# Tanh-weighted gate and product with up on VectorE, weight alone on GpSimd, transposes and key projection moved

## What is computed

```python
x = x + attn(layernorm(x))        # q, k, v projections, softmax in a band of 64, output projection
h = layernorm(x)                  # then the experts:
g = einsum('nh,ehm->enm', h, w_gate)      # 16 experts, 64 hidden
u = einsum('nh,ehm->enm', h, w_up)
inter = silu(g) * u
y_e = einsum('enm,emh->enh', inter, w_down)
y = einsum('ne,enh->nh', combine, y_e)    # combine: routing weight of each token and expert
shared = (silu(h @ sw_gate) * (h @ sw_up)) @ sw_down
x = x + y + shared
```

## Time and profile before

| | |
|---|---|
| median of 3 runs | 814.77 us (814.01 to 815.94) |
| the profiled execution | 814.36 us, span 812.6 us |
| TensorE busy, weight loads | 740.3 us (91%), 611.7 us (75%) |
| GpSimd | 618.8 us (76%) |
| ScalarE | 607.7 us (75%) |
| VectorE | 525.1 us (65%) |
| mean granted clock | 0.977 |
| chain of waits that ended last | PE 45%, POOL 26%, issue 16%, ACT 8% |

### The profile page before, as it was taken

How to read it: one execution, slowest core, us unless ns; L and a number is a source line. 1 busy time by engine, 2 the same in 40 slices (tenths; PEclk the granted TensorE clock), 3 DMA queues, 4 the chain that set the end, 5 groups by cost and what they waited for, 6 DMA issues and landing times.

```text
span 812.6 us, 19809 instructions
## 1 busy us (share of the span) xinstructions
PE 740.3 (91%) x5984; PEld 611.7 (75%) x5984; DVE 525.1 (65%) x1735; ACT 607.7 (75%) x1816; POOL 618.8 (76%) x842
## 2 busy tenths in 40 slices
PE   2568889999999999999999999999999999998876
PEld 1446668787887878787887878787887878786755
DVE  3456686767767676767667676767767575764332
ACT  4787788788787888878788788878787888863332
POOL 3525467879888888978888888988888887956876
PEclk9698899999999999999999999999999999999999
DMA  5000022040413213040312213040313203041321
GB/s 155 26 1 15 14 74 73 15 136 10 120 40 97 63 53 105 2 133 22 105 52 92 65 42 115 2 129 26 105 52 90 67 31 114 3 122 37 117 92 41
DMA packets 50738, 53.86 MB, mean 66 GB/s; under 512 B 5632, under 2 KB 31744, under 8 KB 50560
## 3 DMA queue, kind: packets, MB, share of 16 engines
q1 hardware_dynamic: 50688, 53.25, 21.5%
HBM read 44.31 MB, written 4.72 MB: 60 GB/s over the span
## 4 chain that ended last, share of the span: by engine, by line
PE 45%; POOL 26%; issue 16%; ACT 8%; DMA 2%; DVE 2%; POOLq 1%; SPq 0%; ACTq 0%; DVEq 0%
POOL gate L470 9%; PE PS L1053 8%; PE PS L979 7%; PE PS L869 7%; PE PS L911 6%; PE PS L870 5%; PE PS L871 5%; ACT probs L602 4%; POOL hh L473 4%; POOL q_lo L452 4%; POOL k_lo L462 2%; PE PS L972 2%; PE PS L1050 2%; POOL X L432 1%; PE PS L1014 1%
## 5 line engine op out<-in xcount | busy, mean ns | idle before, releaser
L602 ACT ACTIVATE probs<-PS,neg_max 128x96 f32<-128x96 f32 (+1 forms) x1024 | 245.8, 353 | 60.1 <-DVE neg_max L798 59.4
L470 POOL TENSOR_TENSOR gate<-gate,spread 128x512 f32<-128x512 f32 x128 | 164.2, 1283 | 64.4 <-DMA spread<-weights_by_expert 47.2
L750 DVE STREAM_TRANSPOSE probsT<-probs 128x384 f32<-128x384 f32 (+1 forms) x256 | 124.0, 522 | 101.8 <-ACT probs L602 101.8
L473 POOL TENSOR_TENSOR hh<-gate,tu 128x512 f32<-128x512 f32 x128 | 164.5, 1285 | 17.2 <-POOL gate L470 11.9
L786 DVE SCALAR_TENSOR_TENSOR tu<-th,PS 128x512 f32<-128x512 f32 x128 | 87.9, 687 | 89.3 <-PE PS L871 56.4
L1053 PE MATMUL PS<-wd,hh 128*128 128x128 f32 x1024 | 136.1, 276 | 9.6 <-POOL hh L473 9.6
L1053 PEld LDWEIGHTS PS<-wd,hh 128*128 128x128 f32 x1024 | 126.6, 192 | 15.1 <-POOL hh L473 9.4
L798 DVE TENSOR_REDUCE neg_max<-PS 128x4 f32<-128x384 f32 (+1 forms) x256 | 125.4, 513 | 8.2 <-PE PS L979 5.4
L869 PE MATMUL PS<-x_hi,w_hi 128*128 128x512 f32 x288 | 125.0, 434 | 1.0 <-DVE hs L834 1.0
L560 ACT ACTIVATE th<-PS 128x512 f32<-128x512 f32 x128 | 79.7, 623 | 59.6 <-PE PS L871 59.2
L871 PE MATMUL PS<-x_lo,w_hi 128*128 128x512 f32 x288 | 114.5, 397 | 0.0
(11 more groups left out here) (108 smaller groups left out, 1362.1 us busy)
## 6 DMA issues: line engine op xcount, KB each, us to landing
spread<-weights_by_expert SPq DMA_DIRECT2D x256, 128.0 KB, 3.0
X<-x SPq DMA_DIRECT2D x32, 256.0 KB, 3.4
OUT<-H SPq DMA_DIRECT2D x16, 256.0 KB, 3.0
out<-OUT SPq DMA_DIRECT2D x16, 256.0 KB, 3.1
probsT<-w_gu SPq DMA_DIRECT2D x1, 1152.0 KB, 8.0
wd<-w_down SPq DMA_DIRECT2D x1, 512.0 KB, 9.0
weights_by_expert<-cT SPq DMA_DIRECT2D x16, 32.0 KB, 1.6
probsT<-w_att SPq DMA_DIRECT2D x1, 264.0 KB, 3.5
```

Source lines behind the costliest of these rows:

```text
L470: tt(gate2[:, :], gate[:, k % 2, :], spread[:, k % SP_BUFS, :], ALU.mult).then_inc(s_g2, 1)
L473: tt(hh[:, k % 2, :], gate2[:, :], tu[:, k % 2, :], ALU.mult).then_inc(s_h, 1)
L602: ins = nc.scalar.activation(probs[:, u % 2, tt, a, j0:KW], PS[:, tt, a * KW + j0:a * KW + KW], ACT.Exp, bias=neg_max[:, tt, a:a + 1])
L750: ins = v_.transpose(probsT[:, b, :, t0 + tt, c0:3, :].rearrange("p g c q -> p g (c q)"), probs[:, u % 2, tt, :, c0 * Q:KW])
```

## The change

The pair's activation is split in another way. ScalarE doesn't copy the gate any more. VectorE computes fa = (th + 1) * gate, reading the gate from PSUM, and then tu = fa * up, reading up from PSUM. GpSimd multiplies once: hh = tu * spread. The tiles `gate` and `gate2` and their semaphores go, and with them TensorE's wait on `s_gate`; `s_fa` now counts every pair, and ScalarE waits on it before it writes `th` again.

In step 3 TensorE computes the shared experts' gate and up ahead of the weights' transposes instead of behind them; ScalarE's tanh of the shared experts and its copy to `cT` change places in the same way.

The key projection is done once for both sequences, in step 6, into a whole bank (512 columns); `kr_hi` and `kr_lo` become twice as wide, and the uses of the shared banks go from 15 to 14 in a slot.

```diff
-KP = (6, 8)
+KP = 6
@@ gpsimd, the pair
-                        pool.wait_ge(s_gate, g.n * NP + k + 1)
                         pool.wait_ge(s_spread[k % SP_BUFS], spread_turn(g, k))
-                        tt(gate2[:, :], gate[:, k % 2, :], spread[:, k % SP_BUFS, :], ALU.mult).then_inc(s_g2, 1)
-                        pool.wait_ge(s_g2, g.n * NP + k + 1)
                         pool.wait_ge(s_tu, g.n * NF + k + 2)
-                        tt(hh[:, k % 2, :], gate2[:, :], tu[:, k % 2, :], ALU.mult).then_inc(s_h, 1)
+                        tt(hh[:, k % 2, :], tu[:, k % 2, :], spread[:, k % SP_BUFS, :], ALU.mult).then_inc(s_h, 1)
@@ scalar, the pair
                         act.wait_ge(s_g, g.n * NF + k + 2)
+                        act.wait_ge(s_fa, g.n * NF + k + 1)
                         nc.scalar.activation(th[:, :], PS[:, 4, :], ACT.Tanh, scale=0.5).then_inc(s_th, 1)
-                        copy(gate[:, k % 2, :], PS[:, 4, :]).then_inc(s_gate, 1)
@@ vector, the pair
-                        dve.wait_ge(s_th, g.n * NF + k + 2)
-                        dve.wait_ge(s_u, g.n * NF + k + 2)
-                        v_.scalar_tensor_tensor(tu[:, k % 2, :], th[:, :], 1.0, PS[:, 5, :], ALU.add,
-                                                ALU.mult).then_inc(s_tu, 1)
+                        f = g.n * NF + k + 2
+                        dve.wait_ge(s_th, f)
+                        v_.scalar_tensor_tensor(fa[:, :], th[:, :], 1.0, PS[:, 4, :], ALU.add,
+                                                ALU.mult).then_inc(s_fa, 1)
+                        dve.wait_ge(s_fa, f)
+                        dve.wait_ge(s_u, f)
+                        v_.tensor_tensor(tu[:, k % 2, :], fa[:, :], PS[:, 5, :], ALU.mult).then_inc(s_tu, 1)
@@ tensor, gate_up
-                if not (g.fixed and g.n * NP + f <= 1):
-                    pe.wait_ge(s_gate, g.n * NP + max(f - 1, 0))
@@ tensor, keys: one call in place of keys(0) and keys(1)
-                            exact3(bank[:, 0:T], *w2(WK), xT_hi[:, r], xT_lo[:, r]).then_inc(s_filled[side], 1)
+                        exact3(bank, *w2(WK), xT_hi[:, :], xT_lo[:, :]).then_inc(s_filled[side], 1)
@@ tensor, step 3
+                    g, _ = at(sl, s, SH)
+                    if g:
+                        gate_up(g, NP, 0)
+
                     g, _ = at(sl, s, CT)
...
-                    g, _ = at(sl, s, SH)
-                    if g:
-                        gate_up(g, NP, 0)
-
-                    keys(1)
```

More of the change, by code:

```diff
@@ L187, in preln_block_kernel @@
         q_lo = sb("q_lo", [P, NSB, 4, Q], F32R)
-        kr_hi = sb("kr_hi", [P, T], F32R)
-        kr_lo = sb("kr_lo", [P, T], F32R)
+        kr_hi = sb("kr_hi", [P, TOK], F32R)
+        kr_lo = sb("kr_lo", [P, TOK], F32R)
         k_hi = sb("k_hi", [P, HG, TOK], F32R)
@@ L223, in preln_block_kernel @@
         fa = sb("fa", [P, TOK])
-        gate = sb("gate", [P, 2, TOK])
         tu = sb("tu", [P, 2, TOK])
@@ L542, in slot @@
                         copy(w_hi[:, WG:W_COLS], stage[:, WG:W_COLS]).then_inc(s_cst, 1)
-                    def keys(b):
-                        g, _ = at(sl, s, KP[b])
-                        if g:
-                            side, bank = filled(act, sl, s, KEY_PLACE[b])
-                            if not (g.fixed and g.n == 0 and b == 0):
-                                act.wait_ge(s_k_hi, g.n * GB + b)
-                            copy(kr_hi[:, :], bank[:, 0:T]).then_inc(s_high[side], 1)
-                    keys(0)
+                    g, _ = at(sl, s, KP)
+                    if g:
+                        side, bank = filled(act, sl, s, EARLY)
+                        if not (g.fixed and g.n == 0):
+                            act.wait_ge(s_k_hi, g.n * GB)
+                        copy(kr_hi[:, :], bank).then_inc(s_high[side], 1)
                     g, _ = at(sl, s, LG)
@@ L566, in slot @@
                         copy(oT[:, :], bank[:, 0:T]).then_inc(s_taken[side], 1)
+                    g, _ = at(sl, s, SH)
+                    if g:
+                        act.wait_ge(s_g, g.n * NF + 1)
+                        if not (g.fixed and g.n == 0):
+                            act.wait_ge(s_fa, g.n * NF)
+                        nc.scalar.activation(th[:, :], PS[:, 4, :], ACT.Tanh, scale=0.5).then_inc(s_th, 1)
                     g, _ = at(sl, s, CT)
@@ L572, in slot @@
                         copy(cT[:, :], bank[0:E, :], scale=0.5 * ROUTE_SCALE).then_inc(s_taken[side], 1)
-                    g, _ = at(sl, s, SH)
-                    if g:
-                        act.wait_ge(s_g, g.n * NF + 1)
-                        if not (g.fixed and g.n == 0):
-                            act.wait_ge(s_fa, g.n)
-                        nc.scalar.activation(th[:, :], PS[:, 4, :], ACT.Tanh, scale=0.5).then_inc(s_th, 1)
-                    keys(1)
                     g, _ = at(sl, s, QP)
@@ L627, in slot @@
                         if g:
[L628 removed]
+                            if b == 0:
+                                taken(act, sl, KP, EARLY)
                             if not (g.fixed and g.n == 0):
@@ L632, in slot @@
                             for a in range(HG):
-                                ins = copy(k_hi[:, a, T * b:T * b + T], kr_hi[:, :].bitcast(F32),
+                                ins = copy(k_hi[:, a, T * b:T * b + T], kr_hi[:, T * b:T * b + T].bitcast(F32),
                                            scale=headrow[:, a:a + 1])
@@ L761, in slot @@
                                      ).then_inc(s_taken[side], 1)
-                    def keys(b):
-                        g, _ = at(sl, s, KP[b])
-                        if g:
-                            side, bank = high_out(sl, s, KEY_PLACE[b])
-                            if not (g.fixed and g.n == 0 and b == 0):
-                                dve.wait_ge(s_k_lo, HG * (g.n * GB + b))
-                            split_low(kr_lo[:, :], bank[:, 0:T], kr_hi[:, :]).then_inc(s_taken[side], 1)
                     g, _ = at(sl, s, YE)
@@ L775, in slot @@
                                          ALU.add).then_inc(s_y, 1)
-                    keys(0)
+                    g, _ = at(sl, s, KP)
+                    if g:
+                        side, bank = high_out(sl, s, EARLY)
+                        if not (g.fixed and g.n == 0):
+                            dve.wait_ge(s_k_lo, HG * g.n * GB)
+                        split_low(kr_lo[:, :], bank, kr_hi[:, :]).then_inc(s_taken[side], 1)
                     g, _ = at(sl, s, LN1)
@@ L923, in free @@
                         return use.bank, PS[:, RING[use.bank], :]
-                    def keys(b):
-                        g, _ = at(sl, s, KP[b])
-                        if g:
-                            side, bank = free(KEY_PLACE[b])
-                            r = slice(T * b, T * b + T)
-                            exact3(bank[:, 0:T], *w2(WK), xT_hi[:, r], xT_lo[:, r]).then_inc(s_filled[side], 1)
-                    keys(0)
+                    g, _ = at(sl, s, KP)
+                    if g:
+                        side, bank = free(EARLY)
+                        exact3(bank, *w2(WK), xT_hi[:, :], xT_lo[:, :]).then_inc(s_filled[side], 1)
                     g, _ = at(sl, s, VP)
```

22 lines of the change are left out of this document (7 added, 15 removed).

## The result

| | before | changed |
|---|---|---|
| median | 814.44 us (4 runs, 814.01 to 815.94) | 883.07 us (4 runs, 880.42 to 891.53) |
| ratio to before, 95% interval | | 1.086 (1.078 to 1.093) |
| profiled execution | 814.36 us, span 812.6 us | 880.42 us, span 878.6 us |
| one full slot | 46.0 us | 49.1 to 50.4 us, two of 54.03 and 58.07 |
| mean granted clock | 0.977 | 0.948 |

The change costs 8.6%. I had forecast 854 us and a range up to 872: the direction and the path (the chain that ends at SH) were right, the loss was 29 us larger (27 in the profiled execution), and the measured time lies above the range.

The account below looks back on a forecast made before the run. TensorE's 45.0 us a slot bounds before; afterwards a VectorE and ScalarE chain of 48.3. Profiled 814.4 us, plus 28.1 for slots and ends, plus 11 for the clock, gives 853.5, or 854 against the median; range 834 to 872.

Parts of the forecast that it names:

- the chain that ends at SH: Work alternating between VectorE and ScalarE until tu of step 3 lets TensorE start the shared experts' gate product.
- TensorE bounds by 45.0 us: Kernel before: TensorE's own work is 45.0 of a 46.0 us slot; the VectorE and ScalarE path is nearly as long.
- 0.72 for each of six steps: VectorE's added gate product delays tu, both maxima, exponentials and the next tanh by 0.72 us in steps 5 to 2.
- The chain of 48.3 us: Summed links between starts of the shared experts' gate product: slot 48.3 us instead of 46.0, +2.3.
- F: In each step, the stretch from a tanh to the first exponential, through fa, tu and maximum: 2.55 us.
- tanh to fa 0.64: In each step, VectorE's fa starts 0.64 us after ScalarE's tanh starts, as read from 383.93 to 384.57.
- 0.24: Step 6, ScalarE: the high key copy, widened to 512 columns, takes about 0.5 us instead of 0.26, adding 0.24.
- The clock: Longer waits before the shared experts' gate product lower TensorE's granted clock, costing +11 us over 13 slots.
- half of the slots: Half of 13 slots lose 1.7 us each to the lower clock; bounds none and 22 us.
- The bank uses per slot go from 15 to 14; I see no use that becomes later by it.: One-piece key projection: fewer shared bank uses per slot, no later use seen, no cost put down.
- The transposes behind SH: +0.35.: Step 3: weights' transposes now follow the shared experts' gate product instead of filling the wait, adding 0.35 us a slot.
- The emptying end: -3.5.: Behind the attention's end, the 1.65 us wait for comb and the low clock after it go: about -3.5 us.

Follow-up runs that it names:

- no_gate_product: Changed kernel, slots 6 to 13 written out, VectorE's gate product left out of the routed experts' hidden values: 803.57 us, ratio 0.987.
- after_pair_first: Changed kernel, slots 6 to 13 written out, second-sequence k_hi copies behind step 3's tanh, VectorE's fa and tu ahead of the exponentials' transposes there: 841.87 us.
- after_noloop: Changed kernel with slots 6 to 13 written out and only the last pair in the loop: 873.62 us, ratio 1.072.
- pair_only: Kernel before with only the new pair's activation (fa and tu on VectorE, one GpSimd multiplication, no gate copy): 843.39 us, ratio 1.036.
- after_ct_first: Changed kernel, loop kept, with the weights' transposes back ahead of the shared experts' gate and up: 880.54 us, ratio 1.079.
- keys_only: Kernel before with only the key projection done in one piece: 837.26 us, ratio 1.027.
- order_only: Kernel before with only the shared experts' gate and up moved ahead of the weights' transposes: 822.23 us, ratio 1.010.
- before_noloop: Kernel before with slots 6 to 13 written out and only the last pair in the loop: 811.95 us, ratio 0.997.
- keys_shift: Kernel before with the one-piece key projection, plus ten one-column VectorE writes ahead of everything, restoring its loop body's place: 820.02 us, ratio 1.007.
- extra_ahead: Kernel before, slots 6 to 13 written out, an unused VectorE multiplication per step ahead of tu and both maxima: 875.65 us, ratio 1.076.
- extra_behind: Kernel before, slots 6 to 13 written out, an unused VectorE multiplication per step behind the second maximum: 841.42 us, ratio 1.033.
- before_keys_later: Kernel before, slots 6 to 13 written out, k_hi copies behind step 3's tanh, shared experts ahead of weights' transposes except in the last two slots: 814.95 us.
- transposes_first: Changed kernel, slots 6 to 13 written out, with the weights' transposes back ahead of the shared experts' gate and up: 859.32 us, ratio 1.055.
- after_keys_later: Changed kernel, slots 6 to 13 written out, ScalarE's second-sequence k_hi copies moved behind step 3's tanh: 862.7 us, ratio 1.058.

## Why the prediction came out as it did

- *TensorE bounds by 45.0 us, the chain of VectorE and ScalarE stands just behind it.* Right. Take the gate product away and a slot is TensorE's own 45.1 us and a wait of 0.56 (no_gate_product); shorten the chain without touching the work and the time falls by 32 us (after_pair_first).
- *0.72 for each of six steps.* Right as a mechanism: 4.7 us lie between the slots of after_noloop (50.3) and no_gate_product (45.63). Seven times 0.72 (six steps and the step with SH) would make 5.0, with the clock's fall on top; less shows because without them the chain is shorter than TensorE's work, and a slot can't fall below that.
- *The chain of 48.3 us.* The slot from 671.71 to 720.78, at full clock at both ends, took 49.1: 0.8 more. The term that failed is the first link of F, "tanh to fa 0.64". I had read it in step 3 and used it in every step. In this slot it is 0.96 in step 5 and 0.92 in step 6 (ScalarE, then VectorE):

```profile
680.49 0.60 ACT L551 ACTIVATE th<-PS 128x512 f32<-128x512 f32 x1
...
686.90 0.67 ACT L551 ACTIVATE th<-PS 128x512 f32<-128x512 f32 x1
```

```profile
680.88 0.65 DVE L756 TENSOR_TENSOR OUT<-PS,OUT 128x512 f32<-128x512 f32 x1
681.45 0.67 DVE L773 SCALAR_TENSOR_TENSOR fa<-th,PS 128x512 f32<-128x512 f32 x1
...
687.21 0.69 DVE L653 TENSOR_TENSOR kr_lo<-PS,kr_hi 128x512 fp32r<-128x512 f32 x1 [0.83 <-ACT kr_hi L519]
687.82 0.68 DVE L773 SCALAR_TENSOR_TENSOR fa<-th,PS 128x512 f32<-128x512 f32 x1
```

VectorE is still at the output sum when the tanh of step 5 is there, and in step 6 at `kr_lo`, which part 3 made twice as wide (0.42 in pair_only, 0.69 here). I had priced part 3 in ScalarE's queue, and rightly (from `kr_hi` at 686.43 to the tanh behind it are 0.47, forecast 0.5), and had put it at nothing in VectorE's. So the steps 5 to 3 took 36.65 instead of 36.1; the other 0.2 lie ahead of and behind them. Part 3's share shows between pair_only and after_ct_first, both with the loop: 35.95 and 36.42, 0.47 where I had 0.24. 0.8 us make 10 us in 13 slots.
- *The clock.* Mechanism right, and "half of the slots" was close: it fell in 5 of 12. Such a slot has its tanh of step 5 at 10.25 instead of 8.78 behind the transposes, 1.5 later, and takes 50.3 to 50.4 where the next one is at full clock again: 1.2 net instead of my 1.7. The Trainium skill, page "TensorE: Matmul & The Clock Gate", section "HAM oscillation — how this bites in real kernels", tells of a fall in every iteration, but for longer waits than this one; I was wrong to take it as a rule for every slot here. By the traces 5 of 12 slots pay behind SH, and in after_noloop, with a wait as long, 9 of 13. Over the nine slots without a stall the clock makes 0.7 us a slot (49.8 against 49.1), some 8 us of the 11 that I had put down.
- *"The bank uses per slot go from 15 to 14; I see no use that becomes later by it."* True of the banks, and the wrong place to look. I read the change as work and order, and not as instructions in memory: it shifts the loop bodies, and two turns of the changed kernel stall. That is a step which the prediction lacked, 9 to 12 us put at nothing, and the surprise of keys_only (17 of its 22 us). The Trainium skill has the matter, on the page "Runtime: NRT & Kernel Launch", section "Instruction fetch mechanics": a taken branch whose target isn't in the window at hand forces a fetch before execution goes on. The traces agree in kind (stalls marked "issue" behind the jump, more instruction packets), and add that a shift of ten instructions can decide.
- *The transposes behind SH: +0.35.* Too small. Undone, they give 14.3 us back: 0.9 a slot on average (49.4 against 50.3), clock included, and the rest in the filling pipeline. In the kernel before it was 7.3 (order_only).
- *The emptying end: -3.5.* Wrong sign, +0.9. I had seen that two waits go, and not that there the gate product sits in a shorter circle. TensorE writes gate and up, tanh, fa, tu, and only then may it write again; each round took 3.1 us (VectorE's rows, then TensorE's; L858 begins a round). The second pair of rows is the same place in no_gate_product, 2.5 us apart.

```profile
858.79 0.69 DVE L773 SCALAR_TENSOR_TENSOR fa<-th,PS 128x512 f32<-128x512 f32 x1 [1.76 <-ACT th L551]
859.52 0.69 DVE L777 TENSOR_TENSOR tu<-fa,PS 128x512 f32<-128x512 f32 x1
```

```profile
857.18 0.48 PE L858 MATMUL PS<-x_hi,w_hi 128*128 128x512 f32 x1
...
860.26 0.50 PE L858 MATMUL PS<-x_hi,w_hi 128*128 128x512 f32 x1 [0.55 <-DVE tu L777]
```

```profile
784.30 0.50 PE L855 MATMUL PS<-x_hi,w_hi 128*128 128x512 f32 x1
...
786.81 0.50 PE L855 MATMUL PS<-x_hi,w_hi 128*128 128x512 f32 x1
```

From the last full slot on, no_gate_product needs 97.4 us, after_noloop 107.9, before_noloop 107.2.

The sum of the misses, in the profiled execution (880.4 less 853.5 = 26.9): start 1.3, first and last full slot 3.3, the stalls 12.5, the eleven slots beyond that 16.4, the end 4.4, less the 11 that I had already put down for the clock. The 16.4 are about 8 of the chain and 8 of the clock.

What stays open: why the clock falls in some slots of equal shape and not in others. And the parts don't add up: pair_only's 28.5, keys_shift's 5.7 and order_only's 7.3 make 41.5, and after_noloop takes 61.7 more than before_noloop. The three are of the form with the loop and these two are not, and the clock falls seldom where one part stands alone (behind one SH of 13 in pair_only); I haven't separated the rest.

## What to carry to other kernels

An engine that is 65% busy can still be the bound: what counts most is whether the new operation stands ahead of the one that others wait for, in every engine's fixed order, and here one VectorE operation per step cost 34 us more or less by its place. Add up such a chain link by link over one period, with both engines' queues at each link, and do the same for the emptying end, where the circle is another one. And when a kernel has a loop, look at its turns for idle time marked "issue", and compare the instruction queues of the two pages, before a difference is put down to the edit.

## What the runs showed of the hardware

**Two readers of SBUF block each other.** The extra multiplication reads both operands from SBUF. Its shortest took 0.65 us in extra_ahead and 0.68 in extra_behind. VectorE and GpSimd in extra_behind:

```profile
410.60 1.27 POOL L472 TENSOR_TENSOR gate<-gate,spread 128x512 f32<-128x512 f32 x1
410.93 1.48 DVE L805 TENSOR_TENSOR pad<-wd 128x512 f32<-128x512 f32 x1
411.94 1.61 POOL L475 TENSOR_TENSOR hh<-gate,tu 128x512 f32<-128x512 f32 x1
```

GpSimd's first ends at 411.87; VectorE's, begun at 410.93, ends at 412.41, nearly as if it had started only then; and GpSimd's next takes 1.61 instead of 1.28 for the same reason. Over the whole kernel the mean of hh rose from 1284 to 1444 ns, and TensorE's wait for `comb` from 14.4 to 23.2 us, some 0.6 of the 1.5 us that the slots of extra_behind are longer. The rest I haven't followed. The Trainium skill, page "SBUF — State Buffer", section "🔬 SBUF: two separate sides", states such a lock for a VectorE operation with two SBUF inputs against a GpSimd one that reads SBUF; these rows agree. The changed kernel's fa and tu each read one operand from PSUM and took 682 and 687 ns beside GpSimd: nothing of this touches the change itself.

**The clock and the length of a bare wait.** The wait ahead of SH in kernels of nearly one shape, and behind how many of them the clock fell: 1.00 us, none (before_keys_later); 0.7 to 1.23, none of 13 (after_pair_first); 1.62, one of 13 (pair_only); 1.69, every second (transposes_first); 2.12, 6 of 12 (after_keys_later); 2.4, 5 of 12, four of whose waits were shorter (changed kernel), and 9 of 13 (after_noloop). The length doesn't decide alone: 1.62 and 1.69 are almost the same. Between after_keys_later and after_pair_first VectorE took up the tanh 0.95 us sooner and the mean slot fell by 1.6 us, from 49.6 to 48.05. And a fall is paid for only where TensorE has no room: in the slot 542.46 to 590.52 of after_pair_first, and in 671.71 to 720.78 of the changed kernel, the clock was at its lower level for 3.4 us in the middle, and neither slot was longer for it.

**Where a loop body lies is worth up to 17 us.** Idle times of 1.4 to 5.8 us at a turn came with ten instructions fewer on VectorE and 51 fewer on TensorE ahead of the loop, and went when they were put back. The place isn't all (two turns of four stall in the changed kernel, four of four in after_ct_first, with the body at the same place), and writing out the loop made even the kernel before 2.4 us faster, though it had no visible stall.
